# One feed-forward block of a transformer kernel: the up bias by a matmul, gelu and scaling on ScalarE from and into PSUM, the output bias added early by GpSimd

## The chip, the cores and the metric

One core of a Trainium2 chip. The metric is the device time of one execution in microseconds; the kernel before has a median of 2234.18 us in 3 runs (2232.45 to 2238.2). Engines are called TensorE (PE, with weight loads as PEld), VectorE (DVE), ScalarE (ACT), GpSimd (POOL) and SyncE (SP).

## The reference, cut to what matters

The program is four layers of attention and feed-forward over 4096 tokens of 128 numbers. The change touches the feed-forward of layer 0 alone, a "BitNet" block with 512 hidden numbers, in float32:

```python
def act_quant_fake(x):
    scale = 127.0 / clip(max(abs(x), axis=-1, keepdims=True), 1e-05)
    return clip(round(x * scale), -128.0, 127.0) / scale
def bitlinear(x, w, b):      # weight_quant_fake: w as -1, 0, 1 times mean(abs(w))
    return einsum('btd,hd->bth', act_quant_fake(x), weight_quant_fake(w)) + b
h = layernorm(x, ln1_g, ln1_b)
h = bitlinear(h, w1, b1)
h = gelu(h, approximate=False)
h = layernorm(h, ln2_g, ln2_b)
h = bitlinear(h, w2, b2)     # the caller has x = x + h
```

## The kernel before

`bit_ffn` (line 905) works on 32 tiles of 128 tokens; a tile has its tokens on the partitions. Each engine has a queue of its own, written out by hand: `pipelined` runs a list of (lead, stage) and, at step s, issues each listed stage for unit s + lead, in the order of the list. Engines meet through counting semaphores. An engine executes its queue in order, so whatever stands behind a waiting instruction waits too.

Setup: `loads` brings in weights and biases by eight DMAs on SP's queue; VectorE makes the weights ternary, TensorE turns them.

Stage A, eight groups g of four tiles. VectorE normalises X into `xh` (`normalise_x`, line 994); GpSimd multiplies by g1 and adds b1n (1076, 1078, x_affined); VectorE (`quantise`) takes the row maxima (1005), forms scale and undo (1006 to 1008), scales and caps (1010, four instructions), clips and rounds by adding MAGIC (1012), and subtracts MAGIC into bf16 `xq` (1014). TensorE turns xq (1149), ScalarE copies it to `xqT` (1100), TensorE multiplies by w1T into the four banks of `psH` (1156, one 128x512 tile in each). VectorE (`bias`, 1020) reads psH, times undo plus b1, into `H`; ScalarE applies gelu in place (1106); VectorE takes statistics (`measure`, 1026). VectorE's order in a step is quantise(g+1), normalise_x(g+2), bias(g), measure(g-1).

Between the stages VectorE and one square root on ScalarE make mean2 and rstd2.

Stage B, sixteen pairs k of tiles. ScalarE normalises H into `hn` (1117, two instructions); GpSimd multiplies by g2 and adds b2n (1086, 1088); VectorE (`quantise_h`) takes maxima (1045), `top2`, `undo2`, `scale2` (1046 to 1048, 128x2 each), scales (1049, 1050) and clips (1051); ScalarE subtracts MAGIC into bf16 `hq` (1124); TensorE turns (1164), ScalarE copies (1129), TensorE multiplies by w2T (1172); VectorE forms y = psY times undo2 plus b2 (1057), adds it to X (1061) and takes the statistics of X for the next layer (1066). VectorE's order is residual(k-2), quantise_h(k), measure_x(k-3); ScalarE's is take_h(k-1), normalise(k+2), to_integers(k).

Of the kernel before, what the change touches and what calls it, by code (L numbers as in the profile page):

```python
# [13 lines left out]
ALU = mybir.AluOpType  # L14
ACT = mybir.ActivationFunctionType
# [6 lines left out]
P = 128  # L22
# [882 lines left out]
def bit_ffn(nc, m, t):  # L905
# [5 lines left out]
    with ExitStack() as own:  # L911
# [12 lines left out]
        b1, g2, b2n = sb("b1", [P, HID0]), sb("g2", [P, HID0]), sb("b2n", [P, HID0])  # L924
# [5 lines left out]
        amax, scale, undo = sb("amax", [P, 4]), sb("scale", [P, 4]), sb("undo", [P, 2, 4])  # L930
        hn = sb("hn", [P, 4, 2, HID0])
        hq, hqT = sb("hq", [P, 2, 2 * HID0], BF16), sb("hqT", [P, 2, 2 * HID0], BF16)
        top2, scale2, undo2, minus = sb("top2", [P, 2]), sb("scale2", [P, 2]), sb("undo2", [P, 4, 2]), sb("minus", [P, 1])
        y = sb("y", [P, 2, D])
        loaded = m.sem("loaded")

        def loads(sp):
            sp.dma_start(w1[:, :, :], t["L0_ffn_w1"].rearrange("(c p) d -> p c d", p=P)).then_inc(loaded, 16)
            sp.dma_start(w2[:, :], t["L0_ffn_w2"]).then_inc(loaded, 16)
            for dst, name in ((g1, "ln1_g"), (b1n, "ln1_b"), (b2, "b2"), (b1, "b1"), (g2, "ln2_g"), (b2n, "ln2_b")):  # L940
                sp.dma_start(dst[:, :], t["L0_ffn_" + name].partition_broadcast(P)).then_inc(loaded, 16)

# [8 lines left out]
        xq_ready, xq_turned, xqT_ready, up_ready, biased, gelued = (m.sem(n) for n in (  # L951
            "xq_ready", "xq_turned", "xqT_ready", "up_ready", "biased", "gelued"))
# [6 lines left out]
        with nc.Block() as block:  # L959
            @block.vector  # L960
            def _(dve):
                chain = Chain(dve, chained)
                dve.memset(ones[:, :], 1.0)
                dve.memset(minus[:, :], -MAGIC)
# [23 lines left out]
                A_LINKS = 5  # L988
# [9 lines left out]
                def quantise(g, u, n):  # L998

                    wait_past(dve, xq_turned, g - 1)  # L1000
                    wait_past(dve, xq_ready, g)
                    dve.wait_ge(x_affined, 2 * g + 2)
                    c = Chain(dve, chained, before + A_LINKS * g)
                    x = xh[:, u, :, :]
                    c.link(dve.tensor_reduce(amax[:, :], x, AX.X, ALU.max, apply_absolute_value=True))
                    c.link(dve.tensor_scalar(amax[:, :], amax[:, :], EPS, 1.0 / 127.0, ALU.max, ALU.mult))
                    dve.tensor_scalar(undo[:, u, :], amax[:, :], wmean[:, 0:1], None, ALU.mult)
                    c.link(dve.reciprocal(scale[:, :], amax[:, :]))
                    for j in range(4):
# [6 lines left out]
                def bias(g, u, n):
                    for j in range(4):
                        i = 4 * g + j
                        dve.wait_ge(up_ready, i + 1)
                        dve.scalar_tensor_tensor(H[:, bass.ds(i, 1), :].rearrange("p a h -> p (a h)"), psH[:, j, :], undo[:, u, j:j + 1], b1[:, :],  # L1020
                                                 ALU.mult, ALU.add).then_inc(biased, 1)
# [6 lines left out]
                pipelined(dve, G, [(1, quantise), (2, normalise_x), (0, bias), (-1, measure)])  # L1028
                c = Chain(dve, chained, before + A_LINKS * G)
                c.link(dve.memset(y[:, 0, 0:1], 0.0))  # L1030
# [4 lines left out]
                dve.memset(y[:, 0, 0:1], 0.0).then_inc(r_in, 1)  # L1035
                before_b = c.base + c.n
                B_LINKS = 5

                def quantise_h(k, s, n):

                    dve.wait_ge(affined, 2 * k + 2)
                    wait_past(dve, rounded, k)
                    c = Chain(dve, chained, before_b + B_LINKS * k)
                    h = hn[:, s, :, :]
                    c.link(dve.tensor_reduce(top2[:, :], h, AX.X, ALU.max, apply_absolute_value=True))
                    c.link(dve.tensor_scalar(top2[:, :], top2[:, :], EPS, 1.0 / 127.0, ALU.max, ALU.mult))
                    dve.tensor_scalar(undo2[:, s, :], top2[:, :], wmean[:, 1:2], None, ALU.mult)
                    c.link(dve.reciprocal(scale2[:, :], top2[:, :]))
                    c.link(dve.tensor_scalar(hn[:, s, 0, :], hn[:, s, 0, :], scale2[:, 0:1], 127.0, ALU.mult, ALU.min))
                    c.link(dve.tensor_scalar(hn[:, s, 1, :], hn[:, s, 1, :], scale2[:, 1:2], 127.0, ALU.mult, ALU.min))  # L1050
                    dve.tensor_scalar(h, h, -128.0, MAGIC, ALU.max, ALU.add).then_inc(rounded, 1)

                def residual(k, s, n):
                    dve.wait_ge(down_ready, k + 1)
                    wait_past(dve, x_added, 2 * k)
                    for j in range(2):
                        last = dve.scalar_tensor_tensor(y[:, j, :], psY[:, s % 2, j * D:j * D + D], undo2[:, s, j:j + 1], b2[:, :], ALU.mult, ALU.add)
                    last.then_inc(x_added, 1)
                    dve.wait_ge(x_added, 2 * k + 1)
                    tiles = m.X[:, bass.ds(2 * k, 2), :]  # L1060
                    dve.tensor_tensor(tiles, tiles, y[:, :, :], ALU.add).then_inc(x_added, 1)
# [31 lines left out]
            def _(act):  # L1093
# [15 lines left out]
                pipelined(act, G, [(1, take), (0, gelu)])  # L1109
# [21 lines left out]
                pipelined(act, PAIRS, [(-1, take_h), (2, normalise), (0, to_integers)], period=4)  # L1131

            @block.tensor
            def _(pe):
# [22 lines left out]

                pipelined(pe, G, [(0, up), (1, turn)])
# [1242 lines left out]
def lay_out(inputs):  # L2401
# [7 lines left out]
    t["rms_scale_col"] = np.ascontiguousarray(np.tile(t.pop("L0_xattn_rms_scale"), HEADS).reshape(P, 1))  # L2409
    t["c_ident"] = np.eye(P, dtype=np.float32)  # L2410
# [37 lines left out]
```

## Time and profile before

The profiled execution took 2232.57 us, its span 2230.8 us.

| stretch (us of the span) | what it is |
|---|---|
| 350.6 to 367.0 | loads, statistics, ternary weights |
| 367.0 to 445.1 | stage A |
| 445.1 to 447.3 | statistics between the stages |
| 447.3 to 583.1 | stage B |
| 584.0 on | next layer |

Over the whole span PE is busy 1669.4 us (75%), DVE 1540.4 (69%), ACT 825.1 (37%), POOL 874.6 (39%). In the timeline an engine's line gives start, duration, what it writes and reads, and in brackets how long the engine was idle before it and who ended that. "x4" is four instructions merged; its duration runs from the first start to the last end. PEclk is TensorE's granted clock, 1.00 for 2.4 GHz and 0.50 for 1.2 GHz.

### The profile page before, as it was taken

The page shows a single profiled execution, that of the slowest core. Times are in us where ns is not written, and L with a number is a line of the kernel's source. Part 1 is how long each engine was busy: PE and PEld are TensorE (multiplying, and loading weights), DVE is VectorE, ACT ScalarE, POOL GpSimd, SP SyncE. Part 2 cuts the span into 40 slices and gives each one's busy share as a digit, 9 for nine tenths or more (in the row PEclk, how much of TensorE's full clock was granted, in tenths as well). Part 3 has the DMA queues.
Part 4 walks back from the last instruction along what each step waited for, and adds up shares of the span by engine and source line. Part 5 has one row for each costly group of instructions (what it writes and reads, how often), then busy time and mean ns, then how long its engine had stood idle before and what let it go on. Part 6 is the DMA issues. An engine that isn't in the chain of part 4 may idle for free. (4 is left out here: it accounts for less than half of the span.)

```text
span 2230.8 us, 48391 instructions
## 1 busy us (share of the span) xinstructions
PE 1669.4 (75%) x14912; PEld 1187.2 (53%) x14915; DVE 1540.4 (69%) x3682; ACT 825.1 (37%) x1795; POOL 874.6 (39%) x1058
## 2 busy tenths in 40 slices
PE   3999962212499898996898699918999799358993
PEld 2777651011377665664677344417777577335552
DVE  4999976989677753437677899874555687863332
ACT  1544441344355422322564588700000465122221
POOL 1888841266144243005442000005554343027783
PEclk9999976555599889997898899958999799555555
DMA  3222200000000051111001477416774000424446
GB/s 111 68 66 66 65 17 28 0 0 1 7 1 0 16 162 42 40 36 40 1 0 34 151 311 297 198 37 224 282 265 161 7 0 1 120 47 81 81 83 143
DMA packets 178711, 183.56 MB, mean 82 GB/s; under 512 B 101378, under 2 KB 163650, under 8 KB 171202
## 3 DMA queue, kind: packets, MB, share of 16 engines
q1 hardware_dynamic: 154770, 111.88, 16.2%
q10 hardware_dynamic: 9520, 55.94, 7.1%
q0 software_dynamic: 14336, 14.69, 3.6%
q8 instruction: 42, 0.69, 0.1%
q14 instruction: 43, 0.35, 0.1%
HBM read 107.39 MB, written 72.45 MB: 81 GB/s over the span
## 5 line engine op out<-in xcount | busy, mean ns | idle before, releaser
L748 DVE TENSOR_REDUCE at_mx<-at_psS 128x16 f32<-128x1024 f32 x96 | 117.6, 1225 | 93.7 <-PE at_psS L653 93.7
L711 ACT ACTIVATE at_ET<-at_psT 128x512 f32<-128x512 f32 x192 | 114.6, 597 | 172.3 <-PE at_psT L662 171.7
L1922 POOL TENSOR_TENSOR gr_work<-gr_ring 128x512 f32<-128x512 f32 x96 | 121.7, 1280 | 104.3 <-DVE gr_work L1958 97.2
L617 POOL TENSOR_TENSOR at_KM<-at_K,at_mask 128x512 f32<-128x512 f32 x96 | 100.0, 1042 | 154.0 <-ACT at_Q L698 154.0
L2011 PEld LDWEIGHTS gr_psY<-gr_wd,gr_work 128*128 128x128 f32 x1024 | 134.8, 196 | 39.2 <-DVE gr_work L1958 22.8
L388 POOL TENSOR_TENSOR at_E<-at_Z,at_mx 128x512 f32<-128x512 f32 x128 | 130.9, 1044 | 50.1 <-DVE at_mx L513 50.1
L2011 PE MATMUL gr_psY<-gr_wd,gr_work 128*128 128x128 f32 x1024 | 142.4, 283 | 10.7 <-DVE gr_work L1958 10.6
L662 PE MATMUL at_psT<-kept_ident,at_Z 128*128 128x128 f32 x768 | 127.3, 289 | 9.6 <-DVE at_Z L761 4.6
L1844 PE MATMUL gr_psV<-kept_xT,gr_wu 128*128 (+1 forms) x256 | 125.9, 592 | 0.8 <-ACT gr_V L1713 0.8
L249 ACT ACT_TABLE_LOAD x6 | 7.7, 1283 | 314.7 <-PEq L63 299.3
L675 PE MATMUL at_psO<-at_VZ,at_ET 128*64 128x18 f32 x3072 | 106.9, 212 | 15.6 <-ACT at_ET L711 4.2
L675 PEld LDWEIGHTS at_psO<-at_VZ,at_ET 128*64 128x64 f32 x3072 | 97.3, 138 | 34.1 <-ACT at_ET L711 34.1
L2246 POOL DMA_INDIRECT cap_acc<-cap_Y,cap_idx x64 | 102.0, 1593 | 20.8 <-issue 19.6
L1958 DVE TENSOR_TENSOR gr_work<-gr_psF,gr_work 128x512 f32<-128x512 f32 x128 | 85.7, 685 | 35.3 <-PE gr_psY L2011 20.0
L662 PEld LDWEIGHTS at_psT<-kept_ident,at_Z 128*128 128x128 f32 x768 | 81.4, 142 | 53.3 <-issue 37.3
L2285 DVE TENSOR_TENSOR cap_h<-cap_psU,cap_sg 64x128 f32<-64x128 f32 x64 | 18.1, 283 | 119.9 <-ACT cap_sg L2299 119.9
L1923 POOL MEMSET gr_one<- 64x1 f32 x1 | 0.1, 93 | 255.6 <-POOLq L1688 255.6
L2240 POOL DMA_INDIRECT cap_GX<-cap_rows,cap_idx x64 | 63.4, 991 | 91.1 <-DVE cap_idx L2279 76.8
L1844 PE MATMUL gr_psV<-kept_xT,gr_wg 128*128 (+1 forms) x192 | 98.0, 592 | 0.0
L1724 ACT ACTIVATE gr_ring<-gr_psV,gr_bu 128x512 f32<-128x512 f32 x128 | 88.0, 688 | 21.5 <-PE gr_psV L1844 21.5
L763 DVE TENSOR_TENSOR at_Z<-at_psS,at_mx 128x512 f32<-128x512 f32 x128 | 82.5, 686 | 8.6 <-DVE at_mx L748 3.2
L1164 PE MATMUL bit_psT<-kept_identb,bit_hq 128*128 128x128 bf16 x128 | 16.5, 310 | 93.6 <-ACT bit_hq L1124 93.6
(554 smaller groups left out, 4631.9 us busy)
## 6 DMA issues: line engine op xcount, KB each, us to landing
gr_spill<-gr_ring SPq DMA_DIRECT2D x28, 1792.0 KB, 5.7
gr_ring<-gr_spill ACTq DMA_DIRECT2D x28, 1792.0 KB, 7.2
at_amask<-mask_Bx16xSxS_ff SPq DMA_DIRECT2D x128, 128.0 KB, 2.9
cap_acc<-cap_zero SPq DMA_DIRECT2D x2, 2112.0 KB, 12.6
cap_sums<-cap_acc SPq DMA_DIRECT2D x8, 512.0 KB, 7.2
ex_xs<-ex_zero SPq DMA_DIRECT2D x1, 2496.0 KB, 11.1
ex_row<-ex_xs SPq DMA_DIRECT2D x39, 64.0 KB, 1.8
ex_ys<-ex_out SPq DMA_DIRECT2D x39, 64.0 KB, 1.6
```

The lines of the kernel that those rows point to most:

```text
L388: pool.tensor_tensor(E[:, a, :].rearrange("p (v k) -> p v k", k=SEQ), Z[:, s % 2, a, :].rearrange("p (v k) -> p v k", k=SEQ), mx[:, s % 2, ...
L617: pool.tensor_tensor(KM[:, s, :, :], K[:, s, :].unsqueeze(1).broadcast_to([P, 4, P]), mask4[:, :].unsqueeze(2).broadcast_to([P, 4, P]), AL ...
L662: last = pe.transpose(psT[:, r * P:r * P + P], Z[:, a, r * P:r * P + P], m.ident[:, :])
L675: last = pe.matmul(psO[rows, t * PW:t * PW + PW], ET[:, 4 * a + r, rows], VZ[:, PAIRS * b + t, :, :].rearrange("p j w -> p (j w)"), start= ...
L711: act.activation(ET[:, 4 * a:4 * a + 4, :].rearrange("p r q -> p (r q)"), psT[:, :], ACT.Exp, scale=QK_SCALE).then_inc(exped, 1)
L748: dve.tensor_reduce(mx[:, :].rearrange("p (g v) -> p g v", v=4), psS[:, :, 0:256].rearrange("p g (v k) -> p g v k", k=SEQ), AX.X, ALU.max) ...
L1724: act.activation(ring[:, u, j % TILES, :], psV[:, j % 4, :], ACT.Silu if is_up else ACT.Identity, bias=bias).then_inc(taken, 1)
L1844: pe.matmul(psV[:, j % 4, :], w, x, start=True, stop=True).then_inc(multiplied, 1)
L1922: pool.tensor_tensor(tp[:, s % 4, :], ring[:, s // 4, first, :], ring[:, s // 4, first + 1, :], ALU.mult).then_inc(pooled, 1)
L1958: dve.tensor_tensor(h[:, s % 2, :], psF[:, s % 4, :], product_of, ALU.mult).then_inc(h_ready, 1)
L2011: last = pe.matmul(psY[:, j, :], h[:, s % 2, j * P:j * P + P], wd[:, s, :], start=False, stop=(s == C - 1), skip_group_check=True)
L2246: pool.indirect_dma_start(accs[s % ACCS], bass.IndirectOffsetOnAxis(ap=idx2[:, s:s + 1], axis=0), Y[:, s % 4, :], None, compute_op=ALU.add ...
```

## The change

In stage A the up bias becomes a second matmul into the same psH bank: the stationary operand is `invT`, four rows of 1/undo (turned by TensorE, copied from psY by ScalarE), the moving one `b1_rows`, a float32 constant that has b1 in row j and zeros elsewhere. ScalarE's gelu reads psH with undo as its scale. Scaling by `scale` and adding MAGIC moves to ScalarE (`to_scale`), clipping stays on VectorE. In stage B ScalarE scales from hn into two banks of psH (`to_scale_h`), VectorE clips there in place; `top2` and its limit lie in a third bank. GpSimd adds b2 to X in stage A, so that `residual` becomes one instruction for each tile. Orders change as the lists show.

```diff
-        b1, g2, b2n = ...            # SBUF; the broadcast load of b1 (256 KB) goes
+        b1_rows = sb("b1_rows", [4, 4, HID0])      # loaded last by one DMA, 32 KB
+        inv, invT = sb("inv", [P, 2, 4]), sb("invT", [4, 2, P])
+        h_int = psH[:, 0:2, :]
+        top2, limit2 = psH[:, 2, 0:2], psH[:, 2, 2:4]
 # VectorE, stage A
-                    for j in range(4):
-                        last = dve.tensor_scalar(xh[:, u, j, :], xh[:, u, j, :], scale[:, j:j + 1], 127.0, ALU.mult, ALU.min)
-                    c.link(dve.tensor_scalar(x, x, -128.0, MAGIC, ALU.max, ALU.add))
-                def bias(g, u, n): ...
+                def find_scale(g, u, n):       # waits: xq_turned g - 1, gelued 4 * (g - 1), x_affined 2 * g + 2
+                    ...                        # 1005 to 1008 as before, scale with two buffers
+                    dve.tensor_scalar(inv[:, u, :], scale[:, u, :], winv[:, 0:1], None, ALU.mult).then_inc(scale_ready, 1)
+                def clip(g, u, n):
+                    dve.wait_ge(scaled, g + 1)
+                    c.link(dve.tensor_scalar(x, x, MAGIC + 127.0, MAGIC - 128.0, ALU.min, ALU.max))
                     dve.tensor_scalar(xq[:, u, :], ..., MAGIC, None, ALU.subtract).then_inc(xq_ready, 1)
-                pipelined(dve, G, [(1, quantise), (2, normalise_x), (0, bias), (-1, measure)])
+                pipelined(dve, G, [(1, find_scale), (2, normalise_x), (-1, measure), (1, clip)])
 # VectorE, stage B
+                def find_scale_h(k, s, n):
+                    c.link(dve.tensor_reduce(top2, hn[:, s, :, :], AX.X, ALU.max, apply_absolute_value=True))
+                    c.link(dve.tensor_scalar(limit2, top2, EPS, 1.0 / 127.0, ALU.max, ALU.mult))
+                    dve.tensor_scalar(undo2[:, s, :], limit2, wmean[:, 1:2], None, ALU.mult)
+                    dve.reciprocal(scale2[:, s % 2, :], limit2).then_inc(scale2_ready, 1)
+                def clip_h(k, s, n):
+                    dve.wait_ge(scaled2, k + 1)
+                    dve.tensor_scalar(h_int, h_int, MAGIC + 127.0, MAGIC - 128.0, ALU.min, ALU.max).then_inc(rounded, 1)
                 def residual(k, s, n):
+                        last = dve.scalar_tensor_tensor(mine, psY[...], undo2[:, s, j:j + 1], mine, ALU.mult, ALU.add)  # mine: tile of X
-                    dve.tensor_tensor(tiles, tiles, y[:, :, :], ALU.add).then_inc(x_added, 1)
+                dve.wait_ge(b2_added, G)
+                pipelined(dve, PAIRS, [(0, find_scale_h), (-2, residual), (-3, measure_x), (0, clip_h)], period=4)
 # GpSimd, end of affine_x
+                    pool.tensor_tensor(tiles, tiles, row(b2), ALU.add).then_inc(b2_added, 1)
 # ScalarE
                 def take(g, u, n):
+                    act.activation(invT[:, u, :], psY[0:4, u, 0:P], ACT.Copy)
+                def to_scale(g, u, n):
+                    act.wait_ge(scale_ready, g + 1)
+                    for j in range(4):
+                        last = act.activation(xh[:, u, j, :], xh[:, u, j, :], ACT.Identity, bias=plus[:, 0:1], scale=scale[:, u, j:j + 1])
+                    last.then_inc(scaled, 1)
-                        act.activation(H[:, i, :], H[:, i, :], ACT.Gelu).then_inc(gelued, 1)
+                        act.activation(H[...], psH[:, j, :], ACT.Gelu, scale=undo[:, u, j:j + 1]).then_inc(gelued, 1)
+                pipelined(act, G, [(0, take), (1, to_scale), (0, gelu)])
+                def to_scale_h(k, s, n):       # waits: scale2_ready k + 1, hq_ready k
+                    for j in range(2):
+                        last = act.activation(psH[:, j, :], hn[:, s, j, :], ACT.Identity, bias=plus[:, 0:1], scale=scale2[:, s % 2, j:j + 1])
+                    last.then_inc(scaled2, 1)
+                pipelined(act, PAIRS, [(0, to_scale_h), (-1, take_h), (2, normalise), (0, to_integers)], period=4)
 # TensorE
+                    pe.transpose(psY[0:4, u, 0:P], inv[:, u, :], m.ident[:, :]).then_inc(xq_turned, 1)
-                        wait_past(pe, biased, 4 * g + (j - 3))
+                        wait_past(pe, gelued, 4 * g + (j - 3))
+                        pe.matmul(psH[:, j, :], xqT[:, u, j * D:j * D + D], w1T[:, :], start=True, stop=False)
+                        pe.matmul(psH[:, j, :], invT[:, u, :], b1_rows[:, j, :], start=False, stop=True).then_inc(up_ready, 1)
-                pipelined(pe, G, [(0, up), (1, turn)])
+                pipelined(pe, G, [(0, turn), (0, up)])
```

## Rows read from the trace of the kernel before

**Rows 1.** Windows of stages A, B, one step each: engines busy (instructions), PEclk, DMA share, GB/s
```profile
367.04:445.11 78.07, 22.78 (x63) 6.03 (x64) 70.98 (x178) 26.72 (x42) 20.32 (x16) 0.50 0.00 0
447.32:583.14 135.82, 33.08 (x256) 24.67 (x256) 121.49 (x192) 57.12 (x64) 75.45 (x32) 0.50 0.00 0
388.67:397.68 9.01, 3.04 (x8) 0.76 (x8) 8.84 (x23) 3.04 (x6) 2.55 (x2) 0.50 0.00 0
471.55:487.46 15.91, 4.14 (x32) 3.09 (x32) 15.49 (x23) 7.05 (x9) 9.41 (x5) 0.50 0.00 0
```
**Rows 2.** Timeline of stage A, one steady step, VectorE and GpSimd: start us, duration us
```profile
388.67 2.72 DVE L1020 SCALAR_TENSOR_TENSOR bit_H<-bit_psH,bit_undo,bit_b 128x512 f32<-128x512 f32 x4
388.84 1.28 POOL L1076 TENSOR_TENSOR bit_xh<-bit_xh,bit_g 128x512 f32<-128x512 f32 x1 [4.31 <-DVE bit_xh L994]
...
391.31 2.46 DVE L1026 BATCH_NORM_STATS2 bit_stats<-bit_H 128x6 f32<-128x512 f32 x4
...
393.69 0.67 DVE L1005 TENSOR_REDUCE bit_amax<-bit_xh 128x4 f32<-128x512 f32 x1
...
394.94 0.88 DVE L1010 TENSOR_SCALAR bit_xh<-bit_xh,bit_scale 128x128 f32<-128x128 f32 x4
395.85 0.43 DVE L1012 TENSOR_SCALAR bit_xh<-bit_xh 128x512 f32<-128x512 f32 x1
...
396.65 1.11 DVE L994 TENSOR_SCALAR bit_xh<-kept_X,kept_mean,bit_R 128x128 f32<-128x128 f32 x4
```
**Rows 3.** Timeline of stage B, two pairs: VectorE, GpSimd, ScalarE
```profile
471.43 2.42 POOL L1088 TENSOR_TENSOR bit_hn<-bit_hn,bit_b2n 128x1024 f32<-128x1024 f32 x1
471.55 1.21 DVE L1045 TENSOR_REDUCE bit_top<-bit_hn 128x2 f32<-128x1024 f32 x1
...
473.91 2.26 DVE L1047 TENSOR_SCALAR bit_undo<-bit_top,bit_wmean 128x2 f32<-128x2 f32 x1
...
476.27 2.58 DVE L1049 TENSOR_SCALAR bit_hn<-bit_hn,bit_scale 128x512 f32<-128x512 f32 x1
478.88 0.49 DVE L1050 TENSOR_SCALAR bit_hn<-bit_hn,bit_scale 128x512 f32<-128x512 f32 x1
...
480.13 1.15 ACT L1124 ACTIVATE bit_hq<-bit_hn,bit_minus 128x1024 bf16<-128x1024 f32 x1 [6.61 <-DVE bit_hn L1051]
...
482.40 1.02 ACT L1129 ACTIVATE bit_hqT<-bit_psT 128x1024 bf16<-128x1024 bf16 x1 [1.12 <-PE bit_psT L1164]
...
483.32 1.51 ACT L1117 ACTIVATE bit_hn<-bit_H,bit_shift,bit_rstd 128x512 f32<-128x512 f32 x2
```
**Rows 4.** Timeline of TensorE elsewhere: float32 matmuls of 512 columns, two instructions each
```profile
796.10 1.91 PE L1252 MATMUL ex_psG<-kept_xT,ex_wg 128*128 128x512 f32 x2
797.80 1.92 PE L1251 MATMUL ex_psU<-kept_xT,ex_wu 128*128 128x512 f32 x2
...
1259.72 1.88 PE L1844 MATMUL gr_psV<-kept_xT,gr_wu 128*128 128x512 f32 x4
```
**Rows 5.** Lines 1973 and 518, VectorE reading PSUM: ns min/median/max, first and last start
```profile
L1973 DVE SCALAR_TENSOR_TENSOR kept_X<-gr_psY,gr_r,kept_X x32: 341/343/352, 1540.6 to 1728.8; 128x128 f32 x20, 128x128 f32<-128x128 f32 x12
...
L518 DVE RECIPROCAL at_rs<-at_psO x64: 240/257/259, 58.7 to 313.0; 128x16 f32<-128x16 f32 x64
```
**Rows 6.** Groups by line and shape, whole span: busy us, mean ns, idle before
```profile
L2168 DVE TENSOR_SCALAR cap_F<-cap_psE,cap_slot 128x2048 f32<-128x2048 f32 x1 | 2.3, 2344 | 0.0
...
L1724 ACT ACTIVATE gr_ring<-gr_psV,gr_bu 128x512 f32<-128x512 f32 x128 | 88.0, 688 | 21.5 <-PE gr_psV L1844 21.5
...
L705 ACT ACTIVATE at_VZ<-at_psP,kept_half_mask 128x128 f32<-128x128 f32 x192 | 61.7, 374 | 7.2 <-PE at_psP L639 0.5
```
**Rows 7.** Windows in three other stages, for the clock; columns as in rows 1
```profile
328.00:330.00 2.00, 0.86 (x5) 0.67 (x4) 1.02 (x2) 0.00 (x0) 0.00 (x0) 0.85 0.00 0
335.00:350.00 15.00, 7.15 (x56) 6.39 (x56) 11.15 (x34) 2.39 (x4) 0.00 (x0) 1.00 0.00 1
2020.00:2060.00 40.00, 36.01 (x110) 22.93 (x110) 14.52 (x83) 11.21 (x37) 32.05 (x25) 0.50 0.45 81
```

More of the change, by code:

```diff
@@ L929, in bit_ffn @@
         xh, xq, xqT = sb("xh", [P, 2, 4, D]), sb("xq", [P, 2, 4 * D], BF16), sb("xqT", [P, 2, 4 * D], BF16)
-        amax, scale, undo = sb("amax", [P, 4]), sb("scale", [P, 4]), sb("undo", [P, 2, 4])
+        amax, scale, undo = sb("amax", [P, 4]), sb("scale", [P, 2, 4]), sb("undo", [P, 2, 4])
+        inv, invT = sb("inv", [P, 2, 4]), sb("invT", [4, 2, P])
         hn = sb("hn", [P, 4, 2, HID0])
         hq, hqT = sb("hq", [P, 2, 2 * HID0], BF16), sb("hqT", [P, 2, 2 * HID0], BF16)
-        top2, scale2, undo2, minus = sb("top2", [P, 2]), sb("scale2", [P, 2]), sb("undo2", [P, 4, 2]), sb("minus", [P, 1])
-        y = sb("y", [P, 2, D])
+        scale2, undo2 = sb("scale2", [P, 2, 2]), sb("undo2", [P, 4, 2])
+        plus, minus, spare = sb("plus", [P, 1]), sb("minus", [P, 1]), sb("spare", [P, 1])
         loaded = m.sem("loaded")
@@ L939, in loads @@
             sp.dma_start(w2[:, :], t["L0_ffn_w2"]).then_inc(loaded, 16)
-            for dst, name in ((g1, "ln1_g"), (b1n, "ln1_b"), (b2, "b2"), (b1, "b1"), (g2, "ln2_g"), (b2n, "ln2_b")):
+            for dst, name in ((g1, "ln1_g"), (b1n, "ln1_b"), (b2, "b2"), (g2, "ln2_g"), (b2n, "ln2_b")):
                 sp.dma_start(dst[:, :], t["L0_ffn_" + name].partition_broadcast(P)).then_inc(loaded, 16)
+            sp.dma_start(b1_rows[:, :, :], t["b1_rows"]).then_inc(loaded, 16)
         layer_norm(nc, m, "ln1", to_xT=False, also=loads)
@@ L963, in _ @@
                 dve.memset(ones[:, :], 1.0)
+                dve.memset(plus[:, :], MAGIC)
                 dve.memset(minus[:, :], -MAGIC)
@@ L987, in _ @@
                 before = chain.n
-                A_LINKS = 5
+                A_LINKS = 4
                 def normalise_x(g, u, n):
@@ L1013, in quantise @@
-                    assert c.n == A_LINKS
-                    dve.tensor_scalar(xq[:, u, :], x.rearrange("p j d -> p (j d)"), MAGIC, None, ALU.subtract).then_inc(xq_ready, 1)
[L1016 to L1021, printed above, removed]
+                    c.link(dve.reciprocal(scale[:, u, :], amax[:, :]))
@@ L1043, in quantise_h @@
                     c = Chain(dve, chained, before_b + B_LINKS * k)
[L1044 to L1049, printed above, removed]
@@ L1053, in residual @@
+                    dve.reciprocal(scale2[:, s % 2, :], limit2).then_inc(scale2_ready, 1)
+                def clip_h(k, s, n):
+                    dve.wait_ge(scaled2, k + 1)
+                    dve.tensor_scalar(h_int, h_int, MAGIC + 127.0, MAGIC - 128.0, ALU.min, ALU.max).then_inc(rounded, 1)
                 def residual(k, s, n):
                     dve.wait_ge(down_ready, k + 1)
-                    wait_past(dve, x_added, 2 * k)
                     for j in range(2):
-                        last = dve.scalar_tensor_tensor(y[:, j, :], psY[:, s % 2, j * D:j * D + D], undo2[:, s, j:j + 1], b2[:, :], ALU.mult, ALU.add)
+                        mine = m.X[:, bass.ds(2 * k + j, 1), :].rearrange("p a d -> p (a d)")
+                        last = dve.scalar_tensor_tensor(mine, psY[:, s % 2, j * D:j * D + D], undo2[:, s, j:j + 1], mine, ALU.mult, ALU.add)
@@ L1078, in affine_x @@
                     pool.tensor_tensor(xh[:, u, :, :], xh[:, u, :, :], row(b1n), ALU.add).then_inc(x_affined, 1)
+                    tiles = m.X[:, bass.ds(4 * g, 4), :]
+                    pool.tensor_tensor(tiles, tiles, row(b2), ALU.add).then_inc(b2_added, 1)
                 peeled(pool, G, affine_x)
@@ L1104, in gelu @@
                         i = 4 * g + j
-                        act.wait_ge(biased, i + 1)
-                        act.activation(H[:, i, :], H[:, i, :], ACT.Gelu).then_inc(gelued, 1)
+                        act.wait_ge(up_ready, i + 1)
+                        act.activation(H[:, bass.ds(i, 1), :].rearrange("p a h -> p (a h)"), psH[:, j, :], ACT.Gelu, scale=undo[:, u, j:j + 1]).then_inc(gelued, 1)
                 act.wait_ge(wT_ready, 1)
-                pipelined(act, G, [(1, take), (0, gelu)])
+                pipelined(act, G, [(0, take), (1, to_scale), (0, gelu)])
                 act.wait_ge(r_in, 2)
@@ L1123, in to_integers @@
                     wait_past(act, hq_turned, k - 1)
-                    act.activation(hq[:, s % 2, :], hn[:, s, :, :].rearrange("p j h -> p (j h)"), ACT.Identity, bias=minus[:, 0:1]).then_inc(hq_ready, 1)
+                    act.activation(hq[:, s % 2, :], h_int.rearrange("p j h -> p (j h)"), ACT.Identity, bias=minus[:, 0:1]).then_inc(hq_ready, 1)
                 def take_h(k, s, n):
@@ L2409, in lay_out @@
     t["rms_scale_col"] = np.ascontiguousarray(np.tile(t.pop("L0_xattn_rms_scale"), HEADS).reshape(P, 1))
+    t["b1_rows"] = np.zeros((4, 4, HID0), np.float32)
+    for j in range(4):
+        t["b1_rows"][j, j] = t["L0_ffn_b1"]
+    t.pop("L0_ffn_b1")
     t["c_ident"] = np.eye(P, dtype=np.float32)
```

42 lines of the change are left out of this document (17 added, 25 removed).

## The prediction

> **What bounds the kernel now.** I read the page's busy shares first, to see that no engine is full over the whole span, then windows over the two stages and over one steady step of each, then the timeline inside a step. Stage A lasts 78.1 us and stage B 135.8 us, 214 us together; nothing outside them is touched except the loads [rows 1]. The reader is to see in both stages that VectorE is the full engine: 8.84 of 9.01 us in a step of A and 15.49 of 15.91 us for two pairs of B, where ScalarE has 3.04 and 7.05, GpSimd 2.55 and 9.41, TensorE 3.04 and 4.14 [rows 1]. But the two are full for different reasons. In A VectorE works: bias 2.72, statistics 2.46, scaling 0.88 and so on, each at its own length [rows 2]. In B it is held: the 128x2 multiply of line 1047 takes 2.26 us and the scaling of 1049 takes 2.58, while the same scaling in line 1050 just after takes 0.49. Each long one ends with a GpSimd multiply of about 2.4 us; the maxima of 1045 ran 1.21 us beside one without being held [rows 3]. So in B a VectorE operation from SBUF to SBUF of this kind stands still while GpSimd works, and one that only reduces does not.
>
> **Stage A, the VectorE step.** What stays: maxima and small operations from 393.69 to 394.94, 1.25 us, of which 0.67 is the reduction; normalise 1.03 (396.65 to the end of the step at 397.68); statistics 2.38 (391.31 to 393.69); clip and subtract 0.80 (395.85 to 396.65) [rows 1, 2]. What is added is `inv`, a fourth small operation at (1.25 - 0.67)/3 = 0.2. What goes is bias 2.72 and scaling 0.88. That is 5.7 us of work. GpSimd now has three multiplies or adds in a row, 3 x 1.28 = 3.9 us plus gaps, from 0.1 us after normalise [rows 2]. Beside them lie the statistics (not held) and then the clip's two operations, SBUF to SBUF: the first waits for the second GpSimd operation, the second for the third, and the clip ends some 4.3 us after normalise in place of 3.2. Step: 1.45 + 1.03 + 4.3 = 6.8 us against 9.0. If the clip is not held it is 5.7.
>
> **Stage A, the other loop.** ScalarE's queue is take(g), to_scale(g+1), gelu(g), and TensorE's is turn(g), up(g). Behind take, which waits for turn, stand all gelus; take(g+1) itself stands behind the last gelu. So one loop is: last gelu, take, four up tiles, last gelu. Gelu from PSUM with a pointer I take at 0.65, near the 0.688 of a 512-wide operation from PSUM with a pointer; take is 0.6 plus the small copy, at most 0.37, together 0.95 [rows 6]. The trace has no 4-row stationary operand; the nearest rows are float32 matmuls of 512 columns with full rows: two instructions, 0.43 us each at 2.4 GHz (four in 1.88) and 0.85 each at 1.2 GHz (1.70 between starts of two) [rows 4]. I take these, since a moving operand of 512 columns is what is read; the bounds are nothing and these. The bf16 matmul before it lies between nothing and one such instruction; I take half of one. A tile is then 1.07 us fast or 2.13 slow, four are 4.3 or 8.5, and the loop with 0.2 for hand-overs is 6.1 or 10.3 us. ScalarE's own sum, 0.95 + to_scale 4 x 0.4 + gelu 4 x 0.62 = 5.0, is below both; to_scale (128 wide, by the 0.37 row) ends 3.3 us into the step, before clip needs it at 4.9. The turned `inv` and the b1_rows load (eighth of eight DMAs, 32 KB for 256 KB) are hidden in these waits; I give them nothing.
>
> So the clock decides which loop rules. Stage A is at 0.50 throughout now [rows 1]. Elsewhere it rose after a dense burst: 0.85 in 328 to 330, and then stayed at 1.00 with TensorE 48% busy [rows 7]. An up burst of 8.5 us without a gap is denser than anything in stage A before. I therefore expect it to rise within the first group and VectorE's 6.8 us to rule.
>
> Stage A as a whole: until find_scale(2) starts 19 us (two groups pass normalise, GpSimd, maxima, scaling, clip one after the other, and the first up burst is half slow); five steps of 6.8 = 34; the last group 15 (find 1.45, statistics 2.4, clip 0.9, turn and take 1.6, up 4.3, gelu 0.7, statistics 2.4, hand-overs). 68 against 78.1: **10 us off**.
>
> **Stage B.** VectorE per pair: maxima 1.21 plus three small operations, together 1.9 (as 1.25 in A with a reduction twice as wide). They now read PSUM and must not be held by GpSimd. Nearest rows: a reciprocal from PSUM beside a stage in which GpSimd multiplied too, never over 259 ns in 64; and the very form of the new residual, X from psY and X, never over 352 ns in 32 [rows 5]. I take them as free. The residual is 0.7, statistics of X 0.5, clip of 1024 from PSUM by the 2048-wide row (2344 ns) 1.25 [rows 6]. Sum 4.35, against 7.95 now.
> ScalarE per pair: to_scale_h 1.51 (as line 1117), take_h 1.02, normalise 1.51, to_integers 1.15, total 5.2, with hand-overs 5.3 [rows 3]. No row shows ScalarE or VectorE writing to PSUM; I take SBUF's durations, with bounds from no change to the threefold (below).
> GpSimd per pair: two of 2.35, 4.7 [rows 3].
> What is late next is a loop through all three: normalise(k+2) ends 4.05 us into ScalarE's step k (after to_scale_h and take_h), GpSimd takes 4.75, VectorE 1.9, hand-overs 0.2, and then to_scale_h(k+2) may start. 10.9 us for two steps, 5.45 a pair, just over ScalarE's 5.3. clip_h waits for to_scale_h, and the next find_scale_h stands behind it: it ends 2.8 us into the step, GpSimd's result comes at 3.7, so that costs nothing. to_scale_h(k+1) also waits for to_integers(k), on its own queue.
> Head: step 3 starts 24 us after the first normalise; twelve steps of 5.45 bring to_scale_h(15) to 89.4; its scaling, clip, rounding, turn, copy, matmul, residual and statistics are 8.5. Total 98 against 135.8: **38 us off**. GpSimd's extra adds lie in A, and the wait for all of them is over when B begins.
>
> The Trainium skill speaks against one part: in "ScalarE: Activation LUTs", "Rules for kernel authors", multiplies and adds belong on VectorE because it is faster per element. The trace agrees on the durations, 0.49 us on VectorE where it was not held [rows 3] and 0.75 (half of 1.51) on ScalarE; by the rule each pair would lose 0.5 us and B's gain would be about 30. The loop above has ScalarE's price in it already.
>
> **Sum.** 2232.57 - 10 - 38 = 2185 for an execution like the profiled one. The median of the runs shown is 1.6 us above it, so I forecast 2186.
>
> **Rivals.**
> *The clock stays low.* TensorE 36 us busy of 40 left it at 0.50 with 32- and 64-row float32 operands [rows 7], and 4 rows are fewer. For the rise speaks that the burst here has no gaps. Then A's loop is 10.3 us: 21 + 5 x 10.3 + 23 = 96, 18 us more than before; with B's 38 off, 2232.6 + 18 - 38 + 1.6 = 2214. If it rises in each burst and falls between them, a step is near 7.8 and the total 2191; that I count to the forecast.
> *VectorE is held all the same.* The small operations still write undo2 and scale2 to SBUF. If two of them wait for GpSimd, up to 2.3 us each, B's loop is 10.9 + 4.6 = 15.5 for two pairs, the old 15.9 nearly: the change would not do what its third phrase says. About 4 + 10 off, 2220. Rows 5 speak against it.
> *Slower: writing to PSUM is dear.* h_int has one buffer, so to_scale_h(k), clip_h(k), to_integers(k) and the next to_scale_h are one after the other: 1.51 + 1.25 + 1.15 + 0.2 = 4.1 a pair now hidden under 5.45. If a write to PSUM lengthened the first two by a factor f, it would decide at 2.76 f + 1.35 > 5.45 (f 1.5), eat all of A's and B's gain at 7.95 + 10/16 = 8.6 (f 2.6), and at 3 the pair takes 9.6: 16 x 1.65 = 26 more, 10 less, 2250. Nothing shows such a write, nothing shows a reason for it.
>
> **How the numbers follow.** Forecast 0.60, own range 2179 to 2194 (clip not held in A, five steps of 1.1 us, at the low end; clock up and down at the high end). Low clock 0.27, 2205 to 2216. Still held 0.08. Slow PSUM writes 0.03. The rest, 0.02, is a still better overlap. The range 2178 to 2215 leaves out the held and the slower case and the tails. This kernel's measurement tells about 0.3% (6.7 us) from no change; all but the slow writes, and a mixture of low clock with held VectorE, lie beyond that on the fast side: faster 0.94, same 0.03, slower 0.03.
>
> **What would show it.** PEclk in A: 1.00 from the second group on, and a VectorE step of 6.8; if 0.50 stays, steps near 10.3 with ScalarE's gelu waiting for psH. Clip in A near 0.8 to 1.4 us an operation, ending with GpSimd's operations. In B no small operation over 0.3 us, pairs at 5.45, ScalarE full, GpSimd busy 4.7 of it. to_scale_h at 0.75 each and clip_h at 1.25. If clip_h or to_scale_h is twice that, or the small operations last 2 us, the sum is wrong in B; if a step of A is over 8, it is wrong in A.

## The result, and the profile after

The changed kernel takes 2220.57 us (median of 6 runs, 2213.01 to 2222.63) against 2233.93 (6 runs, 2231.98 to 2238.23): a ratio of 0.9933 (after by before), 95% interval 0.9916 to 0.995. I had forecast 2186, with a range of 2178 to 2215: the sign was right, the size was not, and the time lies above the range. 13 us came where 48 were forecast.

The profiled execution took 2222.42 us, 10.2 less than that of before, so the two traces can be laid side by side. The windows of the changed kernel that answer to [rows 1] (stage A, stage B, a step of A, two pairs of B; columns as there) are these:

```profile
373.60:481.83 108.23, 85.74 (x132) 22.64 (x136) 54.19 (x121) 43.59 (x82) 31.39 (x24) 0.50 0.00 0
484.05:579.10 95.05, 33.11 (x256) 24.69 (x256) 61.45 (x144) 77.79 (x96) 75.03 (x32) 0.50 0.00 0
395.20:407.10 11.90, 11.06 (x19) 2.90 (x19) 6.75 (x15) 5.14 (x10) 3.93 (x3) 0.50 0.00 0
510.63:521.14 10.51, 4.14 (x35) 3.09 (x33) 7.64 (x18) 9.67 (x13) 9.38 (x4) 0.50 0.00 0
```

Stage B did what was forecast: 95.05 for 135.82, 40.8 off. Stage A went the other way: 108.23 for 78.07, 30.2 more. In its step the full engine is no longer VectorE (6.75 of 11.90) but TensorE (11.06), and PEclk is 0.50 (1.2 GHz) in all of it. With 0.5 us more for the loads ahead of A (VectorE waits 5.43 us for the eighth load, `b1_rows`, where it waited 4.93), the block as a whole gives 30.2 + 0.5 - 40.8 = -10.1.

TensorE at the start of stage A, in its first group, in order of time (start, duration):

```profile
387.60 0.61 PE L1172 MATMUL bit_psH<-bit_w1T,bit_xqT 128*128 128x512 bf16 x1
388.14 2.07 PE L1173 MATMUL bit_psH<-bit_b_rows,bit_invT 4*128 4x512 f32 x2
390.14 0.61 PE L1172 MATMUL bit_psH<-bit_w1T,bit_xqT 128*128 128x512 bf16 x1
```

and the loads of its stationary operands:

```profile
387.60 0.10 PEld L1172 LDWEIGHTS bit_psH<-bit_w1T,bit_xqT 128*128 128x128 bf16 x1 [1.50 <-issue]
388.14 0.50 PEld L1173 LDWEIGHTS bit_psH<-bit_b_rows,bit_invT 4*128 4x128 f32 x2 [0.44 <-issue]
390.14 0.10 PEld L1172 LDWEIGHTS bit_psH<-bit_w1T,bit_xqT 128*128 128x128 bf16 x1 [1.50 <-issue]
```

A tile takes 2.54 us (387.60 to 390.14): 0.54 for the bfloat16 matmul and 2.00 for the two float32 instructions of the bias. Each load starts only as the matmul before it ends (388.14 beside 387.60 + 0.61, 390.14 beside 388.14 + 2.07, where the ends are modelled); "issue" is idle time for which the profile shows no wait. ScalarE stands behind it, as the group of waits says (total, times, longest):

```profile
ACT bit_H L1115 <- PE bit_psH L1173: 48.9, 31, 2.8
```

A reader who lays whole traces side by side must know how much they differ where nothing was changed. VectorE's work in the attention's output stage, just ahead of the block, began at 316.9 us before and at 316.5 after, and the block began at 350.67 and 356.75: 6.1 us later through the same code. The 15 us from 330 on, before:

```profile
330.00:345.00 15.00, 7.77 (x61) 6.83 (x61) 10.70 (x32) 2.99 (x5) 0.00 (x0) 1.00 0.00 0
```

and after:

```profile
330.00:345.00 15.00, 10.82 (x47) 9.94 (x48) 6.98 (x22) 2.39 (x4) 0.00 (x0) 0.50 0.00 0
```

The clock had risen at 329 in the one and rose only near 350 in the other. What follows the block was 6.1 us shorter after, the sum of several such shifts. They come and go (the output stage took 33.8 us before, 40.2 after, 35.1 in e1 and 40.3 in e2), so each experiment is read by the block, and its time beside it.

### The profile page after: what moved, and what is told of

It reads as the page before. It is cut to its first block and busy times, and to the rows that moved or that the text cites. A ratio compares the mean times of both kernels' runs of the same rounds, so it can differ in the third digit from the quotient of the medians.

```text
span 2220.6 us, 48488 instructions
## 1 busy us (share of the span) xinstructions
PE 1735.4 (78%) x14981; PEld 1208.6 (54%) x14987; DVE 1463.4 (66%) x3579; ACT 862.7 (39%) x1867; POOL 883.7 (40%) x1066
## 5 line engine op out<-in xcount | busy, mean ns | idle before, releaser
L505 DVE TENSOR_TENSOR at_Z<-at_psS,at_amask 128x512 f32<-128x512 f32 x128 | 81.6, 677 | 7.1 <-PE at_psS L424 7.1
## 6 DMA issues: line engine op xcount, KB each, us to landing
cap_acc<-cap_zero SPq DMA_DIRECT2D x2, 2112.0 KB, 12.6
```

## Experiments

The block runs from ln1's first VectorE instruction to ln2's. In the table "ahead" ends with the copy of `w2T`, A with the last gelu, and B begins with the first normalise; these are starts and ends read from the timelines, in us. (The stage A of the expectations, in which the changed kernel has 108, runs from the first normalise to the last statistics. By that count e1 has 78.9, e2 63.0, e3 67.6, e4 69.8, e5 108.4, e6 108.3 and e8 63.7.)

| kernel | ahead | A | between | B | block | median (runs) |
|---|---|---|---|---|---|---|
| before | 16.5 | 74.0 | 6.3 | 136.7 | 233.4 | 2233.9 (6), 2236.6 beside e1 to e4 (7), 2237.0 beside e5 to e8 (9) |
| changed | 16.9 | 105.7 | 4.7 | 96.0 | 223.3 | 2220.6 (6) |
| e1 B alone | 16.4 | 74.7 | 6.3 | 96.1 | 193.4 | 2191.5 (4) |
| e2 no bias matmul | 17.2 | 60.4 | 4.7 | 96.0 | 178.3 | 2175.0 (4) |
| e3 bias in bf16 | 17.2 | 65.0 | 4.7 | 96.0 | 182.9 | 2181.1 (4) |
| e4 128 rows | 18.0 | 67.2 | 4.7 | 96.1 | 185.9 | 2185.2 (4) |
| e5 64 rows | 18.3 | 105.8 | 4.7 | 96.0 | 224.8 | 2218.2 (1) |
| e6 32 rows | 17.7 | 105.7 | 4.7 | 96.0 | 224.0 | 2223.5 (1) |
| e7 B in SBUF | 16.6 | 105.7 | 4.7 | 123.1 | 250.0 | 2249.6 (6) |
| e8 bf16, 128 rows, loads | 12.6 | 61.1 | 4.7 | 96.0 | 174.4 | 2175.6 (4) |

**e1: stage B's part alone.** Stage A's code is that of before, except that GpSimd's third operation, the addition of b2, is in it. Its main line against the changed kernel, an excerpt:

```diff
-pipelined(dve, G, [(1, find_scale), (2, normalise_x), (-1, measure), (1, clip)])
+pipelined(dve, G, [(1, quantise), (2, normalise_x), (0, bias), (-1, measure)])
```

> Stage A as it was in the kernel before (bias by VectorE from SBUF, quantising on VectorE), stage B as in the changed kernel, with GpSimd's third addition kept in stage A's loop. Theory (stage A's gain and loss are separate from stage B's; A lost 30 us, B gave 41): stage B 95 us, stage A 78 to 86 (the third addition's 1.4 us of GpSimd per step can hold VectorE's instructions), the block from ln1's first VectorE instruction to ln2's about 192 to 200 us against 233.4 before and 223.3 changed, the time 2193 to 2200. Rival (part of B's 41 us comes from stage A's slower, differently ordered hand-over): stage B above 105, time above 2205.

Measured: B 96.1, A 74.7, ratio to the kernel before 0.979 (0.9774 to 0.9807). The two stages add up: B is the same 96 us behind either stage A, and the changed kernel lost in A what e1 does not. The time of 2191.5 is 1.5 under the range expected. The addition of b2 costs A 0.7 us.

**e2: the bias matmul left out.** The output then lacks b1.

```diff
-pe.matmul(psH[:, j, :], xqT[...], w1T[:, :], start=True, stop=False)
-pe.matmul(psH[:, j, :], invT[:, u, :], b1_rows[:, j, :], start=False, stop=True).then_inc(up_ready, 1)
+pe.matmul(psH[:, j, :], xqT[...], w1T[:, :], start=True, stop=True).then_inc(up_ready, 1)
```

> The changed kernel without the four float32 bias matmuls of a step; it leaves the bias b1 out of the output, all else (the turn of the inverse scales, its copy, the order of the queues) stays. Theory (the float32 matmuls at the low clock are what stage A waits for, 2.1 us of each 2.54 us tile): stage A falls from 108 to about 68 to 72 us, bound by VectorE's 6.8 us step, time about 2182 to 2185. Rival 1 (the new order on TensorE's and ScalarE's queues, turn ahead of up and the take in front of gelu, is what costs): the step stays over 8.5 us, stage A over 82, time over 2195. Rival 2 (ScalarE's gelu from PSUM with a scale of its own is the bound): the step stays near 8, stage A about 78, time about 2191.

Measured: A 60.4, 45.3 us less than in the changed kernel, steps of 6.79 to 6.81 (from one group's row maxima to the next, behind the first two), ratio 0.9713 (0.9696 to 0.973). The matmul is the whole loss: without it A is 13.6 us shorter than in the kernel before, so the new order of the queues and gelu from PSUM cost nothing that shows. By the count of the expectation A is 63.0, 5 under its low end, and the time of 2175.0 is 7 under: against e3, which came out about as was expected here, two of the steps are 0.5 us shorter, and what follows the last row maxima takes 12.0 us for 15.6.

**e3: the same matmul in bfloat16.** `invT` is bfloat16, and `b1_rows` is converted once, so both are rounded.

```diff
-pe.matmul(psH[:, j, :], invT[:, u, :], b1_rows[:, j, :], start=False, stop=True)
+pe.matmul(psH[:, j, :], invT[:, u, :], b1_half[:, j, :], start=False, stop=True)
```

> The changed kernel with the bias matmul's two operands in bfloat16 (the copy out of PSUM writes bfloat16, b1's rows are converted once by ScalarE). Theory (the float32 operand makes the matmul four times dearer at the low clock): the bias matmul costs 0.43 us as the bfloat16 one beside it, a tile 0.9 to 1.1, four tiles and the turns under 6.8 us; stage A about 68 to 72 us with VectorE as the bound, time 2182 to 2186, even with the clock at 0.50. Rival (the switch of the stationary operand, 0.5 us before each matmul, is what costs, not the columns): a tile near 1.9, step 9.4, stage A about 90, time about 2203.

Measured: A 65.0, steps of 6.8 and 7.3 in turn, ratio 0.9739 (0.9721 to 0.9757); A (67.6 by the expectation's count) and the time are each just under the range expected. The windows of stage A and of two steps:

```profile
370.79:435.78 64.99, 41.30 (x104) 9.86 (x104) 51.44 (x116) 40.58 (x81) 31.42 (x24) 0.50 0.00 0
403.14:417.30 14.16, 10.39 (x27) 2.50 (x27) 13.46 (x31) 9.90 (x20) 7.88 (x6) 0.50 0.00 0
```

VectorE is the full engine again (13.46 of 14.16) at the low clock. So the change did not need the clock: a bias matmul at about one quarter of the float32 price was enough. The 4-row matmuls are 0.54 us apart in place of 0.43, as each load still waits for the matmul before it (start, duration, idle time before):

```profile
388.76 0.10 PEld L1175 LDWEIGHTS bit_psH<-bit_b_half,bit_invT 4*128 4x128 bf16 x1 [0.44 <-issue]
389.29 0.10 PEld L1174 LDWEIGHTS bit_psH<-bit_w1T,bit_xqT 128*128 128x128 bf16 x1 [0.44 <-issue]
```

The rival of that expectation, that the switch is what costs, is out as the main price: a tile is 1.07 us, not 1.9, and the switch is 0.1 us of each matmul. In float32 the switches are dearer, 0.43 of a tile's 2.54 us, as e4 shows.

**e4, e5, e6: the height of the float32 operands.** Rows of zeros are added; in stage A the instructions and their columns are the same. Ahead of it the zeros are cleared once, and `b1_rows`, now larger, is waited for by TensorE alone and not by VectorE's first sums. An excerpt, the two operands:

```diff
-inv, invT = sb("inv", [P, 2, 4]), sb("invT", [4, 2, P])
+inv, invT = sb("inv", [P, 2, 4]), sb("invT", [P, 2, P])   # e5: 64, e6: 32
-b1_rows = sb("b1_rows", [4, 4, HID0])
+b1_rows = sb("b1_rows", [P, 4, HID0])                     # e5: 64, e6: 32
```

> The changed kernel with the float32 bias matmul kept, but its operands 128 rows tall (rows 4 to 127 are zeros): the same columns, the same instructions, 32 times the rows at work. Theory (operands of 4 rows keep the granted clock at 0.50 in stage A although TensorE is over 90% busy): the clock rises to 1.00 within stage A, a tile costs about 1.1 to 1.3 us, the step is VectorE's 6.8 to 7, stage A 70 to 78 us, time 2183 to 2192. Rival (rows do not matter, the clock stays down for another reason): stage A 105 to 110 us as in the changed kernel, time 2214 to 2222.

> As the run with 128 rows, but the float32 bias matmul's operands are 64 rows tall (rows 4 to 63 zeros). With 4 rows the clock stayed at 0.50 for all of stage A, with 128 it rose to 1.00 within the first group. Theory (it is the share of rows at work that counts, and half of them is too little, as in the last stage of the kernel before, where operands of 32 and 64 rows kept TensorE busy 36 of 40 us at 0.50): stage A stays at 0.50 and takes 95 to 106 us. Rival (only very few rows are too little): the clock rises, stage A 66 to 72 us.

> The same with 32 rows (rows 4 to 31 zeros). Both theories: if 64 rows leave the clock at 0.50, so do 32 (stage A 95 to 106 us, a tile of 2.1 to 2.55 us); if 64 rows raise it and 32 do not, the edge lies between; if both do, only the 4 rows are too few and stage A is 66 to 72 us.

Measured: 128 rows give A 67.2 (ratio 0.9765, 0.9749 to 0.9781), 64 and 32 rows give the 105.7 of 4 rows to within 0.1 us. By the expectations' count e4 is just under its range and e5 and e6 are 2 us over the one for a clock that stays down. Windows of e4, over the start of the first up burst, the rest of it, the next groups, and the one stretch where the clock fell again:

```profile
382.00:385.00 3.00, 2.16 (x4) 0.81 (x4) 2.23 (x9) 2.81 (x7) 1.27 (x2) 0.50 0.00 0
385.00:387.00 2.00, 2.00 (x6) 1.14 (x5) 1.90 (x2) 1.91 (x3) 1.92 (x3) 0.82 0.00 0
387.00:413.00 26.00, 17.94 (x64) 7.63 (x63) 22.71 (x55) 18.22 (x38) 13.00 (x11) 1.00 0.00 1
413.00:416.00 3.00, 3.00 (x6) 1.35 (x5) 2.97 (x6) 1.46 (x4) 2.92 (x3) 0.50 0.00 0
```

and all of stage A in e5:

```profile
369.24:475.01 105.77, 85.80 (x132) 22.76 (x136) 51.71 (x116) 42.34 (x81) 31.41 (x24) 0.50 0.00 0
```

With full-height operands the clock rises within the first group, as I had forecast for the change, and falls for some 3 us once; rows of zeros are enough. With half the rows TensorE is busy 85.80 of 105.77 us and stays at 0.50.

Height is not all that sets the clock. In the attention's output stage of the changed kernel, whose operands all have 128 rows, it stayed at 0.50 from the first matmul at 324.7 us on and rose only near 350, where the same four matmuls shorten from 1.11 to 0.66 us:

```profile
346.86 1.11 PE L874 MATMUL do_psT<-kept_ident,do_On 128*128 128x128 f32 x4 [1.38 <-DVE do_On L819]
347.76 1.91 PE L881 MATMUL do_psY<-do_Wo,do_OT 128*128 128x128 f32 x8
351.06 0.66 PE L874 MATMUL do_psT<-kept_ident,do_On 128*128 128x128 f32 x4 [1.38 <-DVE do_On L819]
```

And behind the block, in the kernel before, it rose (0.50 in 607 to 608, 0.75 in 608 to 609) just after sixteen matmuls of 32 rows between others of 128:

```profile
606.23 1.16 PE L653 MATMUL at_psS<-at_KM,at_Q 32*64 32x256 f32 x16
607.31 0.80 PE L632 MATMUL at_psP<-kept_xT,at_Wq 128*128 128x128 f32 x2
```

So short operands in a stream do not by themselves rule out a rise. What is shown is that in this stage, with the same instructions, 4, 32 and 64 rows left the clock down and 128 did not. The height did a second thing. TensorE and its loads in e4, first tiles, still at the low clock:

```profile
382.90 0.61 PE L1174 MATMUL bit_psH<-bit_w1T,bit_xqT 128*128 128x512 bf16 x1 [0.84 <-ACT bit_xqT L1104]
383.31 1.92 PE L1175 MATMUL bit_psH<-bit_b_rows,bit_invT 128*128 128x512 f32 x2
385.01 0.64 PE L1174 MATMUL bit_psH<-bit_w1T,bit_xqT 128*128 128x512 bf16 x1
```

```profile
382.91 0.74 PEld L1175 LDWEIGHTS bit_psH<-bit_b_rows,bit_invT 128*128 128x128 f32 x2
384.16 0.15 PEld L1174 LDWEIGHTS bit_psH<-bit_w1T,bit_xqT 128*128 128x128 bf16 x1 [0.52 <-issue]
```

Here the loads begin while the matmul before is running (382.91 beside 382.90, 384.16 beside 383.31), and the tile is 2.11 us: 0.41 for bfloat16 and 1.70 for float32, the very price of [rows 4]. So 0.43 us of the changed kernel's tile is weight loading that a full-height operand hides. In words of the Trainium skill ("TensorE: Matmul & The Clock Gate", "Step-by-step: what each phase is for"), a weight load is pulled ahead of running matmuls if the row groups don't conflict or it goes to a background buffer. The runs show that pull for 128 rows behind 128, and not for switches between 128 and 4, 32 or 64 (a float32 pair of 2.00 us in each of the three). The two things came together in e4; no run has one without the other for the whole stage.

**e7: stage B's numbers back in SBUF.** The instructions and their order stay.

```diff
-last = act.activation(psH[:, j, :], hn[:, s, j, :], ACT.Identity, ...)
+last = act.activation(hn[:, s, j, :], hn[:, s, j, :], ACT.Identity, ...)
-dve.tensor_scalar(h_int, h_int, MAGIC + 127.0, MAGIC - 128.0, ALU.min, ALU.max)
+dve.tensor_scalar(hn[:, s, :, :], hn[:, s, :, :], MAGIC + 127.0, MAGIC - 128.0, ALU.min, ALU.max)
```

> The changed kernel with stage B's scaled numbers back in SBUF: ScalarE scales hn in place, VectorE clips hn in place, top2 and limit2 in SBUF. Instructions, their order and their count stay. Theory (the gain of stage B comes from operands in PSUM: VectorE's instructions with SBUF on both sides and GpSimd's additions hold one another, those with PSUM do not): the period of a pair goes from 5.26 back to 6.5 to 8, stage B to 112 to 135 us, the time 16 to 38 us over the changed kernel's 2220. Rival (the gain comes from the work given to ScalarE and from the additions that are gone, whatever the memory): the period stays within 0.3 us of 5.26, stage B 95 to 101, time 2216 to 2227.

Measured: B 123.1, the period 7.0 (13.99 for two pairs), ratio 1.0054 (1.0036 to 1.0073), 0.5% over the kernel before, as A's loss is still in it. The timeline of VectorE and GpSimd:

```profile
509.66 2.38 DVE L1048 TENSOR_SCALAR bit_undo<-bit_tops,bit_wmean 128x2 f32<-128x2 f32 x1
509.67 2.34 POOL L1090 TENSOR_TENSOR bit_hn<-bit_hn,bit_b2n 128x1024 f32<-128x1024 f32 x1
...
513.69 0.69 DVE L1053 TENSOR_SCALAR bit_hn<-bit_hn 128x1024 f32<-128x1024 f32 x1 [0.69 <-ACT bit_hn L1134]
...
518.48 2.35 POOL L1090 TENSOR_TENSOR bit_hn<-bit_hn,bit_b2n 128x1024 f32<-128x1024 f32 x1
...
518.65 2.73 DVE L1053 TENSOR_SCALAR bit_hn<-bit_hn 128x1024 f32<-128x1024 f32 x1 [1.71 <-ACT bit_hn L1134]
```

In every other pair the 128x2 multiply again lasts as long as GpSimd's addition beside it (0.23 in the pairs between), and the clip 2.73, where it takes 0.69 with GpSimd idle (513.69). It was so in the kernel before, where GpSimd had these two beside the long ones of [rows 3], the second an addition and not the multiply that I wrote:

```profile
473.81 2.33 POOL L1086 TENSOR_TENSOR bit_hn<-bit_hn,bit_g 128x1024 f32<-128x1024 f32 x1
476.22 2.34 POOL L1088 TENSOR_TENSOR bit_hn<-bit_hn,bit_b2n 128x1024 f32<-128x1024 f32 x1
```

In the changed kernel the same two steps of VectorE, with PSUM operands, run beside GpSimd at their own length:

```profile
511.38 2.35 POOL L1088 TENSOR_TENSOR bit_hn<-bit_hn,bit_g 128x1024 f32<-128x1024 f32 x1 [0.79 <-ACT bit_hn L1126]
512.09 0.22 DVE L1048 TENSOR_SCALAR bit_undo<-bit_psH,bit_wmean 128x2 f32<-128x2 f32 x1
513.80 2.35 POOL L1090 TENSOR_TENSOR bit_hn<-bit_hn,bit_b2n 128x1024 f32<-128x1024 f32 x1
513.94 1.23 DVE L1053 TENSOR_SCALAR bit_psH<-bit_psH 128x1024 f32<-128x1024 f32 x1 [0.65 <-ACT bit_psH L1134]
```

The clip is dearer in PSUM (1.23) than in SBUF beside an idle GpSimd (0.69), and still cheaper than 0.69 and 2.73 in turn. Of B's 40.7 us, 27.1 come from where the operands lie, given the new sharing of the work, and 13.6 from the work that moved or went. Which of the operands in PSUM counts most was not tried. The Trainium skill's rule ("SBUF — State Buffer", "Who interferes with whom") is that VectorE and GpSimd share a port pair as an exclusive lock; the rows of e7 agree (2.38 beside 2.34), and the changed kernel's, with PSUM operands, escape it (0.22).

**e8: the version that follows.** e3 with operands of 128 rows (zeros cleared on chip), and the first sums waiting for the two weights alone. An excerpt, the wait:

```diff
-dve.wait_ge(loaded, LOADS)
+dve.wait_ge(w_loaded, 32)      # the six vectors are waited for just before stage A
```

> The bfloat16 bias matmul with operands 128 rows tall (rows 4 to 127 zero, cleared on chip), and the weights' two loads on a semaphore of their own, so that the sums of the weights no longer wait for the six vectors. Theory (a full-height operand's weight load hides beside the matmul before it, and a short one's does not: 0.43 instead of 0.54 us per matmul; the loop is VectorE's all the same): step 6.8 to 7.05, the last group 1 us shorter, stage A 62 to 65 us against 65.0 with 4 rows in bfloat16; ahead of it 2 to 5 us less than 17.2 by the loads; time 2172 to 2180. Rival (the vectors' landing is only waited for later, and the loop is as VectorE sets it): 2179 to 2184, no change from 2181.

Measured: 4.6 us less ahead, 3.9 less in A than e3, steps of 6.8, ratio to the kernel before 0.9714 (0.9692 to 0.9736), 2175.6: the fastest that computes everything, 61 us below the kernel before. Of the 3.9 us in A, the hidden loads' share and the clock's (a mean of 0.70 for 0.50, last section) are not told apart.

## Why the prediction was wrong, point by point

- *Stage A, the clock: the step that failed.* "I therefore expect it to rise within the first group." It stayed at 0.50 for 108 us, and with it the float32 bias matmul cost 2.00 us a tile: TensorE's loop of 11.9 us, not VectorE's 6.8, set the step. The rise was taken from a stage with operands of 128 rows [rows 7]; e4 rises where I said, e5, e6 and the changed kernel do not. The row that spoke against it, 36 of 40 us busy at 0.50, stood in the same group, and I gave it 0.27 because this burst had no gaps. I had also read that row too simply, here and in the expectation of e5: its stretch has matmuls of 128 rows in turn with those of 32 and 64, so it never showed short operands alone (rows below, from the kernel before). Idle time alone does not tell the cases apart: the 128-row stage above rose with TensorE idle 1.38 us in each 4.2, this one stayed down with 0.84 idle in 11.9. That the waiting loads of the short operand play no part is argued, not shown, as they came and went with the height. What the chip goes by stays open.

```profile
2031.32 0.69 PE L2327 MATMUL cap_psU<-cap_GT,cap_wgu 128*64 128x128 f32 x2
2031.80 0.63 PE L2328 MATMUL cap_psU<-cap_GT,cap_wgu 128*64 128x128 f32 x2
2032.37 0.79 PE L2333 MATMUL cap_psY<-cap_wdn,cap_h 64*128 64x128 f32 x2
2033.09 0.79 PE L2316 MATMUL cap_psQ<-cap_more,cap_past_end 32*128 32x128 f32 x2
```

- *Stage A, the tile.* The low-clock rival had the mechanism and a tile of 2.13; it is 2.54, since I put the loads of the 4-row operand at nothing (e4's 2.11 shows the 2.13 where they are hidden). Four tiles make 1.64 us a step: 10.3 became 11.9, the stage 108 for 96. With this the rival's 2214 becomes 2214 + 12 - 3 (B), about 2223, for the 2220.6 measured.
- *Stage A, VectorE's step.* Forecast 6.8, and 6.8 in e2 and e8, where VectorE rules; 6.8 and 7.3 in turn in e3. Normalise ends at 396.9 in e3 and the clip at 401.35, 4.4 us later for 4.3; its second operation lasts 1.37, against 0.43 for a like one that was not held [rows 2], and ends just after GpSimd's third operation:

```profile
399.62 1.45 POOL L1080 TENSOR_TENSOR kept_X<-kept_X,bit_b 128x512 f32 x1
...
399.98 1.37 DVE L1024 TENSOR_SCALAR bit_xq<-bit_xh 128x512 bf16<-128x512 f32 x1
```

- *Stage A's queues and ScalarE.* Gelu 0.687 for the 0.65 taken, the copies 0.27 and 0.57 us against 0.95 together; e2 shows no cost of the order itself. Right.
- *Loads: "I give them nothing."* They cost 0.5 us. VectorE's first sums wait for all eight loads; in e8, where they wait for two, the stretch ahead of A is 4.6 us shorter than in e3.
- *Stage B.* Pairs at 5.26 for 5.45 on average, stage 95 for 98. The loop is the one named: the maxima wait for GpSimd's addition, GpSimd for normalise, ScalarE for the scale.

```profile
L1088 POOL TENSOR_TENSOR bit_hn<-bit_hn,bit_g 128x1024 f32<-128x1024 f32 x16 | 37.6, 2348 | 41.9 <-ACT bit_hn L1126 41.9
L1134 ACT ACTIVATE bit_psH<-bit_hn,bit_plus,bit_scale 128x512 f32<-128x512 f32 x32 | 23.7, 772 | 12.9 <-DVE bit_scale L1049 12.0
L1053 DVE TENSOR_SCALAR bit_psH<-bit_psH 128x1024 f32<-128x1024 f32 x16 | 19.7, 1232 | 12.5 <-ACT bit_psH L1134 12.5
L1046 DVE TENSOR_REDUCE bit_psH<-bit_hn 128x2 f32<-128x1024 f32 x16 | 19.6, 1227 | 16.6 <-POOL bit_hn L1090 16.5
L1048 DVE TENSOR_SCALAR bit_undo<-bit_psH,bit_wmean 128x2 f32<-128x2 f32 x16 | 3.5, 219 | 0.6
```

- *The Trainium skill's rule on ScalarE.* By it ("ScalarE: Activation LUTs", "Rules for kernel authors"; its reason, the faster VectorE, is given there for bfloat16, and the numbers here are float32) B's gain was put at about 30. It was 41; what the rule leaves out here is seen in e7, where the same sharing of the work with operands in SBUF gave 13.6.
- *The other rivals.* "VectorE is held all the same": no, the multiply of 2.26 us is 0.22, although it still writes SBUF. "Writing to PSUM is dear": no, ScalarE's 772 ns into PSUM stands beside 801 for normalise in SBUF, and VectorE's clip takes 1.23 us for the 1.25 forecast.
- *The sum.* A was put at -10 and is +30; B at -38 and is -41. The miss of 35 us is A's 40, less 3 from B and some between executions. e4 (2185) comes out where I had put the change, by the path that I had forecast; e3 (2181) comes near it by another, a cheap matmul at the low clock.

Left open: at which height between 64 and 128 rows the two effects turn, which no run here tried, and how much of e4's 38 us each of them is worth beside the estimate of 12 for the loads (108 for 96, above). e5 and e6 were executed once each; their stage A repeats that of the changed kernel to 0.1 us.

## What to carry to other kernels

Before work is given to TensorE "for nothing", price it at the low clock, with its type and its stationary operand's height as they will be, and see whether the engine's sum is still under the loop's; if it isn't, the forecast hangs on the clock. Where a short operand takes turns with full ones, try zero rows up to 128, or bfloat16 where the numbers allow it: the one was worth 38 and the other 41 us of stage A here. Where VectorE and GpSimd work side by side on SBUF, moving operands to PSUM was worth two thirds of the gain in stage B (27.1 of 40.7 us), more than the work taken off VectorE.

## What was not expected of the hardware

- The float32 bias matmul cost the same 2.00 us with 4, 32, 64 rows, and its weight load was hidden in none of the three; at 128 rows it was 1.70 and hidden, at the same clock.
- TensorE busy 85.74 of 108.23 us left the clock at 0.50 with 4 rows; with 128 rows and 42.6 of 67.5 us busy the mean was 0.87:

```profile
371.50:439.00 67.50, 42.63 (x136) 18.45 (x136) 51.77 (x118) 41.29 (x82) 31.48 (x24) 0.87 0.00 0
```

- In bfloat16 the same held on a smaller scale: 0.50 for all of stage A with 4 rows (e3), a mean of 0.70 with 128 (e8):

```profile
366.16:427.22 61.06, 27.30 (x103) 10.26 (x104) 51.28 (x117) 39.45 (x81) 31.42 (x24) 0.70 0.00 0
```
